# Layer 1 of a two-layer decoder: the common list of steps written anew, with spreads two pairs ahead of their scans and in-projections in front of the sums

## The reference

```python
def _mamba2(x, ...):                       # kind M
    zxbcdt = x @ in_proj_w.T               # z | xBC | dt
    xBC = silu(conv4(xBC) + conv_b)        # four taps along the tokens
    dt = softplus(dt + dt_bias)
    dA = exp(dt * -exp(A_log))
    S = dA_t * S + xdt_t B_t ; y_t = S C_t # 8 heads of 64, a scan over the tokens
    y = (y + D * xh) * silu(z)
    y = y * rsqrt(mean(y * y) + 1e-5) * norm_w
    return y @ out_proj_w.T
x = _layernorm(x + _mamba2(x, ...))
# kind X: mLSTM in its parallel form, 4 heads of 64
log_D = cumsum-differences of log_sigmoid(fgate) + igate, causal
C = (q k^T / 8) * exp(log_D - rowmax)
h = C / (max(|rowsum(C)|, exp(-rowmax)) + 1e-6) @ v
x = _layernorm(x + multihead_layernorm(h))
# kind F: FFN with binarized weights
x = _layernorm(x + gelu(x @ bw1.T + b1) @ bw2.T + b2)
```

## Time and profile before

| | |
|---|---|
| runs, median (lowest to highest) | 1498.09 us (1496.36 to 1498.52) |
| the profiled execution | 1499.02 us, its span 1497.3 us |
| TensorE, busy share of the span | 85% (1273.8 us) |
| VectorE, busy share | 56% (836.8 us) |
| ScalarE, busy share | 39% (578.4 us) |
| mean granted clock of TensorE | 0.872 |

### The profile page before, as it was taken

One profiled execution on the slowest core, in us unless ns is written; L12 is line 12 of the kernel. 1 busy time (PEld: TensorE's weight loads), 2 busy tenths in 40 slices (PEclk: granted clock), 3 DMA queues, 4 the chain that ended last, 5 costly groups with the idle time before them and its releaser, 6 DMA issues.

```text
span 1497.3 us, 22724 instructions
## 1 busy us (share of the span) xinstructions
PE 1273.8 (85%) x8404; PEld 1052.2 (70%) x8404; DVE 836.8 (56%) x2630; ACT 578.4 (39%) x1307; POOL 152.1 (10%) x184
## 2 busy tenths in 40 slices
PE   4899999998998998998989957777878977987866
PEld 3678887676887777886778846565667756876755
DVE  5725378654577464687354766336736472656352
ACT  2246342364322473423554234323423532452333
POOL 4996013000000000000000000000010001000000
PEclk9999799999799997999997978578868975996788
DMA  8000001000001000000101110000100000010000
GB/s 326 20 15 2 1 1 43 16 1 1 1 1 44 15 1 1 1 26 19 59 1 36 36 57 0 1 1 0 29 14 1 20 24 1 0 29 14 1 15 14
DMA packets 21388, 33.27 MB, mean 22 GB/s; under 512 B 11424, under 2 KB 12192, under 8 KB 20128
## 3 DMA queue, kind: packets, MB, share of 16 engines
q1 hardware_dynamic: 21280, 31.82, 6.2%
HBM read 27.62 MB, written 4.19 MB: 21 GB/s over the span
## 4 chain that ended last, share of the span: by engine, by line
PE 68%; DVE 20%; ACT 7%; issue 4%; POOL 1%; DVEq 0%; ACTq 0%; POOLq 0%
PE ps L433 39%; PE ps L676 6%; PE ps L574 3%; DVE arena L1701 3%; PE ps L592 2%; PE ps L591 2%; DVE z L1513 2%; PE ps L590 2%; DVE arena L1330 1%; PE ps L566 1%; PE ps L564 1%; DVE pq L1360 1%; PE ps L537 1%; PE ps L550 1%; ACT pq L1031 1%
## 5 line engine op out<-in xcount | busy, mean ns | idle before, releaser
L433 PE MATMUL ps<-wts,arena 128*128 128x256 f32 (+2 forms) x1008 | 215.7, 375 | 2.2 <-ACT arena L1271 2.2
L433 PE MATMUL ps<-arena,wts 128*128 128x256 f16 (+1 forms) x1344 | 190.6, 297 | 20.6 <-ACTq L406 20.6
L433 PEld LDWEIGHTS ps<-wts,arena 128*128 128x128 f32 (+1 forms) x1008 | 164.8, 166 | 45.3 <-ACT arena L1271 3.0
L433 PEld LDWEIGHTS ps<-arena,wts 128*128 128x128 f16 (+1 forms) x1344 | 154.0, 115 | 49.9 <-issue 20.8
L1513 DVE SCALAR_TENSOR_TENSOR z<-ps,small,z 128x256 f32<-128x256 f32 x256 | 123.8, 484 | 41.3 <-PE ps L676 26.8
L676 PE MATMUL ps<-wts,pq 128*128 128x256 f32 x512 | 121.1, 381 | 4.7 <-DVE z L1513 4.7
L1121 ACT ACTIVATE pq<-ps 128x512 f32<-128x512 f32 x72 | 43.0, 597 | 170.7 <-PE ps L433 170.6
L676 PEld LDWEIGHTS ps<-wts,pq 128*128 128x128 f32 x512 | 92.8, 191 | 17.1 <-DVE z L1513 3.2
L574 PE MATMUL ps<-ident,pq 128*128 128x128 f32 x384 | 73.8, 305 | 32.7 <-DVE arena L1430 11.9
L433 PE MATMUL ps<-xT,wts 128*128 128x256 f32 x320 | 88.0, 430 | 10.0 <-DVE arena L1701 10.0
L574 PEld LDWEIGHTS ps<-ident,pq 128*128 128x128 f32 x384 | 46.9, 160 | 58.0 <-ACT arena L999 26.6
(11 more groups left out here) (286 smaller groups left out, 2488.2 us busy)
## 6 DMA issues: line engine op xcount, KB each, us to landing
cT<-in_cT SPq DMA_DIRECT2D x16, 256.0 KB, 2.8
wts<-in_up SPq DMA_DIRECT2D x1, 2304.0 KB, 15.4
wts<-in_down SPq DMA_DIRECT2D x1, 2304.0 KB, 20.4
xT<-in_xT SPq DMA_DIRECT2D x8, 256.0 KB, 4.1
xin<-in_x SPq DMA_DIRECT2D x8, 256.0 KB, 3.0
xmid<-xin SPq DMA_DIRECT2D x8, 256.0 KB, 2.0
wts<-in_w SPq DMA_DIRECT2D x2, 1024.0 KB, 5.0
wts<-in_c SPq DMA_DIRECT2D x16, 128.0 KB, 3.2
```

The lines of the kernel that those rows point to most:

```text
L433: ins = mm(out_, l, r, start=(n == 0), stop=(n == len(pairs) - 1))
```

## The change

The list `WINDOW` is the same hundred steps in another order. In front of the spreads: `in.0.0` goes in front of `dsum.0`, `in.0.2` in front of `gain.0` and `dsum.1` (which moves behind `up.0.0`), `in.0.4` in front of `gain.1`; `zg.0.0` and `zg.0.2` go between the `up`s of s = 1; `down.0` goes behind all `up`s, `down.1` behind `zg.1.2` and `conv.1.2`. In the scan part each `decay` stands two M pairs in front of its `scan`; `cb.1` and `xs.1` go behind the first four spreads of the window; `hidden`, `heads` and `ln5` of both sequences move back, `heads.1` behind `scan.1.3` and the squares, `ln5.1` behind `out.1`; the `sq`s stand in twos. Besides, `in` and `zg` name the mark ("zTa", s, "out") for their `colproj` to wait on, the eviction of the transposed input.

```diff
--- before.py
+++ after.py
@@ -71,15 +71,16 @@
 
 LAG = {"M": 0, "X": 1, "F": 2}
 WINDOW = [(w[0],) + tuple(int(x) if x.isdigit() else x for x in w.split(".")[1:]) for w in """
-    M.load.0 X.ztb.0 M.load.1 X.ztb.1 X.gates.0 M.dt.0 X.gates.1 M.dt.1 F.ztc.0 X.forget.0 M.dsum.0 F.ztc.1 X.forget.1
-    M.dsum.1 F.up.0.0 M.in.0.0 X.gain.0 F.up.0.2 M.in.0.2 X.gain.1 M.csrow.0 F.up.0.4 X.rows.0 M.in.0.4 F.up.0.6
-    X.rows.1 M.csrow.1 M.in.1.0 F.up.1.0 F.up.1.2 X.cols.0 M.in.1.2 F.down.0 F.up.1.4 X.cols.1 F.up.1.6 M.in.1.4
-    M.zg.0.0 M.conv.0.0 M.zg.0.2 M.conv.0.2 M.conv.0.4 F.down.1 M.zg.1.0 M.cb.0 M.xs.0 M.conv.1.0 M.zg.1.2 M.conv.1.2
-    M.conv.1.4 X.nrm.0 X.nrm.1 F.ln6.0 X.cell.0.0 X.score.0.0 F.ln6.1 M.cb.1 M.xs.1 M.decay.0.0 X.cell.0.1 X.read.0.0
-    X.score.0.1 M.scan.0.0 M.decay.0.1 X.cell.1.0 X.read.0.1 X.score.1.0 M.scan.0.1 M.sq.0.0 M.decay.0.2 X.hidden.0
-    X.cell.1.1 X.read.1.0 X.score.1.1 M.scan.0.2 M.decay.0.3 X.read.1.1 X.heads.0 M.scan.0.3 M.decay.1.0 X.hidden.1
-    M.sq.0.2 M.decay.1.1 M.scan.1.0 X.ln5.0 M.rms.0 M.decay.1.2 M.scan.1.1 X.heads.1 M.out.0 M.sq.1.0 M.decay.1.3
-    M.scan.1.2 M.ln4.0 X.ln5.1 M.scan.1.3 M.sq.1.2 M.rms.1 M.out.1 M.ln4.1""".split()]
+    M.load.0 X.ztb.0 M.load.1 X.ztb.1 X.gates.0 M.dt.0 X.gates.1 M.dt.1 F.ztc.0 X.forget.0 M.in.0.0 M.dsum.0 F.ztc.1
+    X.forget.1 F.up.0.0 M.in.0.2 X.gain.0 M.dsum.1 F.up.0.2 M.in.0.4 X.gain.1 M.csrow.0 F.up.0.4 X.rows.0 F.up.0.6
+    M.csrow.1 M.in.1.0 X.rows.1 F.up.1.0 M.zg.0.0 F.up.1.2 X.cols.0 M.in.1.2 M.zg.0.2 F.up.1.4 X.cols.1 F.up.1.6
+    M.in.1.4 F.down.0 M.conv.0.0 M.conv.0.2 M.conv.0.4 M.zg.1.0 M.cb.0 M.xs.0 M.conv.1.0 M.zg.1.2 M.conv.1.2 F.down.1
+    M.conv.1.4 X.nrm.0 X.cell.0.0 X.score.0.0 M.decay.0.0 F.ln6.0 X.nrm.1 X.cell.0.1 M.decay.0.1 X.read.0.0 X.score.0.1
+    M.cb.1 M.xs.1 F.ln6.1 M.decay.0.2 M.scan.0.0 X.cell.1.0 M.scan.0.1 X.read.0.1 M.decay.0.3 X.score.1.0 M.scan.0.2
+    X.cell.1.1 M.decay.1.0 X.hidden.0 M.scan.0.3 X.read.1.0 M.decay.1.1 X.score.1.1 M.sq.0.0 M.sq.0.2 M.scan.1.0
+    M.decay.1.2 X.read.1.1 M.scan.1.1 X.heads.0 M.rms.0 M.decay.1.3 X.hidden.1 M.out.0 M.scan.1.2 X.ln5.0 M.ln4.0
+    M.scan.1.3 M.sq.1.0 M.sq.1.2 X.heads.1 M.rms.1 M.out.1 X.ln5.1 M.ln4.1
+""".split()]
 
 FIRST = ["arow", "nw", ("al", 0), ("al", 1), "al2", ("tr", 0, 0, 0), ("tr", 0, 0, 4), ("tr", 0, 1, 0), ("tr", 0, 1, 4)] + [
     ("tr", 1, cc, 0) for cc in range(FM)]
@@ -909,10 +910,10 @@
                     mamba_dt(*n)
                 if step == "in":
                     s, m = n
-                    colproj(s, "xbc", win[:, :, DI:2 * DI + 2 * DS], xT[s], [], m, m + 2, "c")
+                    colproj(s, "xbc", win[:, :, DI:2 * DI + 2 * DS], xT[s], [("zTa", s, "out")], m, m + 2, "c")
                 if step == "zg":
                     s, m = n
-                    colproj(s, "zg", win[:, :, 0:DI], xT[s], [], m, m + 2, "b")
+                    colproj(s, "zg", win[:, :, 0:DI], xT[s], [("zTa", s, "out")], m, m + 2, "b")
                 if step == "dsum":
                     s = n[0]
                     eng.wait_ge(*pe.at("dA", s))
```

## The result

The changed kernel took 1474.24 us (median, 1473.18 to 1475.06) against 1497.22 us for the kernel before (1493.55 to 1498.52): a ratio of 0.985 [0.983, 0.987], so faster by 23.0 us. The forecast was 1474.5, which is 24.0 less than before.

A forecast was written before the change was run, and what follows sets the result against it. TensorE was taken to bound the fronts, VectorE's work and idle time the scan parts. Scan parts -6.5, -7.7, -11.3, -9.3, windows 4 and 5 -0.5, fronts +0.5, 0, +5.4, +5.4 gave -24.0: about 1474.5 us, range 1466 to 1484.

The forecast's parts named there:

- my own bounds: Limits on scan part gains: -3 to -10 us in window 0, -4 to -16 in the others.
- my own sign: The prediction is wrong if scan parts shorten by under 5 us each or full fronts grow by over 8.
- The fronts: Taps ahead of the sums lengthen TensorE's waits to 5.5 and 5.1 us: +5.4 us in windows 2 and 3.
- The table loads at nothing: Fronts of windows 2 and 3: four more ScalarE table loads each, covered by three projections, costed at nothing.
- Rival 4: Each ScalarE table switch stops it for twice its 1.28 us load, some 4 us a full window: 1482, chance 0.07.
- The scan part: Spreads two pairs ahead bring exps before VectorE needs them; window 2 -11.3 us, window 3 -9.3, window 1 -7.7.
- Window 0: Scan part: eight serial pairs overlap with two in hand, TensorE then the bound: 51.5 to 45, -6.5 us.
- Rival 1: Scan parts: idle time only moves; just `heads.1` and the hidden table load gain: -8, 1490 us, chance 0.18.
- Rival 2: Fronts: taps ahead of the sums and the low clock cost 29 us, making the kernel slower: 1505, chance 0.10.
- Rival 3: Scan parts stay at 2.4 GHz; `rms.1` and `out.1` lose some 4 us in four windows: 1459, chance 0.15.

The follow-up runs named there:

- e4: Changed kernel with `heads.1` alone moved back ahead of `out.0`, `scan.1.2` and `scan.1.3`: 1489.75 us.
- e8: Changed kernel with the split projections of e3 and the idle matmuls of e7 together: 1427.97 us.
- e1: Changed kernel with the first fifty steps (the fronts) back in the old order, scan parts new: 1477.09 us.
- e2: Changed kernel with the last fifty steps (the scan parts) back in the old order, fronts new: 1503.92 us.
- e3: Changed kernel with `in.0.0` and `in.0.2` ahead of the sums on TensorE only, ScalarE's and VectorE's parts behind `dsum.1`: 1447.17 us.
- e5: Changed kernel with `zg.0.0` and `zg.0.2` back behind `down.0`, ahead of their `conv`s, eight table loads fewer in layer 1: 1484.46 us.
- e6: Changed kernel with each `decay` put behind the `scan` of the pair before it, so no M pair in hand: 1502.39 us.
- e9: Kernel of e1 (old fronts, new scan parts) with only `down.1` late, behind `conv.1.2`: 1473.44 us.
- e7: Changed kernel with sixteen idle matmuls in TensorE's wait for the squares ahead of `rms.1`: 1465.61 us.

## Why the prediction was right, point by point

**The sum.** Forecast and measured, in us:

| | w0 | w1 | w2 | w3 | w4, w5 | layer 0 | sum |
|---|---|---|---|---|---|---|---|
| fronts, forecast | +0.5 | 0 | +5.4 | +5.4 | | | +11.3 |
| fronts, measured | +0.7 | +2.3 | +4.7 | +5.8 | | | +13.5 |
| scan parts, forecast | -6.5 | -7.7 | -11.3 | -9.3 | -0.5 | 0 | -35.3 |
| scan parts, measured | -11.2 | -2.5 | -9.7 | -10.4 | -1.8 | -2.0 | -37.6 |

The sum is -24.0 against -24.1, and this closeness is partly luck: window 0 gave 4.7 us more than its term, window 1 5.2 us less, and 2.0 us lie in layer 0, which isn't the change's. Both windows ended outside my own bounds for them (-3 to -10, and -4 to -16). By my own sign, scan parts that shorten by under 5 us each, the working fails for window 1, where it is 2.5 us. In window 0 I had costed waits and not what the clock does once they are gone: the low-clock time fell from 38 to 14 us. In window 1 the idle time that was to go did not: VectorE's idle time for exps, scores and scans went from 13.1 to 15.4 us, the last product of y ended 3 us earlier, which is less than `heads.1` alone, and the low-clock time rose from 24 to 27 us. Why window 1 stays near 60 us in nearly every kernel (59.0 to 62.4; 65.4 in e4, 56.3 in e8) is not settled. It has no `down.1` to lie over the table load, so its first product comes at t = 4.6 (1035.24, against t = 4 in the forecast), and the clock is low behind that; no run moves that start alone.

**The fronts.** This step held in its mechanism and in its numbers. I had waits of 5.5 and 5.1 us ahead of the sums; the rows have 5.40 and 4.99. e1 and e2 confirm the price from both sides (4.5 and 5.6 us less without it, 4.6 and 4.4 us more with it alone), and e3 the cause: the same projections ahead of the same sums, without the taps, take the waits down to 0.67 and 1.16 us. In window 1 I had let the start of the scan part absorb the delay; it did not, by 2.3 us, a size near what can't be told.

**The table loads at nothing.** Right in that there are four more a full window and no wait of TensorE comes of them, not even the 0.2 us at `up.1.6`. Wrong in that I gave the moved `zg`s themselves no value. By e5 they fill a wait and are worth 4.3 us in the front of window 1 and, net of the four loads, some 2.5 in those of windows 2 and 3. Rival 4 is refuted by the rows: ScalarE doesn't stop for longer than the load, and TensorE has no wait there. The Trainium skill's price that spoke for it isn't borne out in this trace.

**The scan part.** The size was right for windows 2 and 3, and one step of its working failed. I had the exps arrive ahead of VectorE's need, so that the idle time at the products falls from 6.5 to 3 us. It is 6.1. In all, VectorE stood idle for 11.2 us between its first and its last product of window 2, where I had 5 to 6. VectorE still meets ScalarE, which works in order, and e6 says that the lead of the M spreads is worth only 0.5 and 3.2 us there. The old list had that lead for s = 1 already, which I had overlooked. What took its place: the wait for scores fell from 3.1 us to none, where I had 0.5; `heads.1` beside the tail brought 4.3 and 5.7 us (e4), not 4.0; and `down.1` over the table load brought 3.1 and 6.1 us (e9 against e1), where I had counted 3.2 from the earlier first product. The last product ends at t = 46.7 where I had 43.5, and the part came out at 55.9, only 1.5 us over my 54.4, because the tail behind that product was 9.5 us and not 10.9. The parts taken one by one don't add up: with the lead they make 7.9 of 9.7 us in window 2 and 15.0 for 10.4 in window 3. Each of them also moves the time at the low clock, and how much of each is that stays open.

**Window 0.** The mechanism, serial pairs that a pair in hand makes overlap, is shown by e6 (waits of 2.15, 2.15 and 1.86 us without the lead). But I had all eight pairs serial in the kernel before. Its trace has waits of 2.15, 2.16, 2.92 and 1.86 us ahead of the scans of s = 0, and 0.58, 0, 0 and 1.61 us ahead of those of s = 1. The term was 4.7 us short because I took "-3 to -10" from TensorE's idle time and left its matmuls at the low clock.

**The rivals.** Rival 1 (idle only moves) was true in window 1 and half true in windows 2 and 3: the exps' idle didn't shrink, but the part got shorter by other means. Rival 2 named the right place: the new order ahead of the sums costs what was said, 4.7 and 5.8 us, under the 8 us from which it would have decided. e2, 1503.9 us, is that rival's world, with the front's cost and without the scan part's gain. Rival 3 came true in part: in windows 2 and 3 the clock was low for 20 and 17 us, where it had been 38 and 31, but the wait of 3.65 us ahead of `rms.1` kept the tail slow. e7 shows the rest of it when the wait is filled.

## What to carry to other kernels

When a step is moved ahead in a list that all engines walk, move only the part of the engine that is idle there. Here the matmuls ahead of the sums were worth some 28 us once ScalarE's and VectorE's part of the same step stayed behind them. Look for a block that needs nothing fresh (`down.1`, `zg`) and put it over a table load or ahead of a wait. Where a wait of TensorE stays ahead of dense work, try idle matmuls in it, and read the time of what follows, not that of the wait.
